# Loading the context already turned, and sharing the first norm between VectorE and ScalarE

## The chip, the cores and the metric

The kernel runs on one core of one Trainium2 chip. The metric is the device time of one execution in microseconds (us). Engines are TensorE (PE in the profile), VectorE (DVE), ScalarE (ACT), GpSimd (POOL) and SyncE (SP); SP and ScalarE both issue DMA transfers here.

## The reference

Four blocks are added to x one after the other. x and the context have shape (8, 256, 512) in float32. Only the start of the first block is touched:

```
def _layernorm(x, axis=-1, eps=1e-05):
    m = jnp.mean(x, axis=axis, keepdims=True)
    v = jnp.var(x, axis=axis, keepdims=True)
    return (x - m) / jnp.sqrt(v + eps)

# block 1: k = v = context, q = layernorm(x), head_dim 8, so 32 heads over the 256 positions
kv = jnp.einsum('bhil,bhjl->bijhl', k_, v_)
y = causal convolution of kv with ssm_kernel[h] along l (512 features), by FFT
out = einsum('bijhl,bhil->bjhl', y + kv * D, q_)
x = x + _L0_xattn_ref(ctx_2048, ctx_2048, _layernorm(x), ssm_kernel, D, 8)
# block 2: expert-choice routing FFN, block 3: retention, block 4: gated FFN with LoRA experts
```

The convolution runs along the 512 features, so x and the context are needed with the features on the partitions, that is, transposed from how they lie in memory.

## The kernel before

x has 2048 tokens, in 16 tiles of 128 tokens by 512 features (`TILES`), handled in 4 groups of 4 (`GROUP`). The stage before the convolution, here called stage A, makes two buffers with the features on the partitions: `ct` (the context) and `qt` (the norm of x). Both are seen as 32 blocks m (four blocks of 128 features times 8 batches) of 256 positions; `head_cols(t, h)` takes the 8 positions of head h from each block.

ScalarE first issues four loads of x, one per group, into `xres`. SP issues the constants, the taps and `d_heads`, then sixteen loads of one context tile each into four buffers `cin`, each when the transposes of the tile four before are done, and behind the first four the write of the taps into `toep`, from which the Toeplitz strips of the convolution are read (`strip_of`). The three first strips and the weights of block 2 (`ewf` and others) are issued behind the last context tile.

For each group TensorE turns four context tiles (banks 0 to 3) and four tiles of `xn` (banks 4 to 7), with `turn`: four transposes of 128x128. ScalarE copies every turned tile out of PSUM, first the four of `ct` and then the four of `qt`. VectorE works the norm of x by groups: `ln_stats` takes the statistics of four tiles (line 286), their aggregates (291) and adds eps (294), then waits until GpSimd has raised the variance to the power -1/2 (`ln_rstd`, line 305); `ln_apply` (299) writes four tiles of `xn`, each when the buffer is free.

At the end of the stage every engine waits for `END_A`: all copies into `ct` and `qt` done. Then ScalarE writes `kx` for heads 0 to 2 and `qx` for head 0 (`doubled`, line 620), GpSimd multiplies `kv` from `kx` (`kv_of`, lines 488 and 491), TensorE runs head after head with 20 products of strip and kv (line 939), ScalarE spreads the result (`spread`), VectorE and GpSimd multiply with `qx` (lines 1366, 1368, 502) and VectorE sums into `qt` (1372). Everything is ordered by semaphores; each engine works its own list in order.

Behind the convolution blocks 2 to 4 follow. The stage just behind it already works its norm by pairs of tiles (`pair`, `pair_root`, `apply`): statistics of two tiles on VectorE, power and product on GpSimd, application on ScalarE (line 669).

Of the kernel before, what the change touches and what calls it, by code (L numbers as in the profile page):

```python
# [13 lines left out]
F32 = mybir.dt.float32  # L14
F32R = mybir.dt.float32r
I32 = mybir.dt.int32
ALU = mybir.AluOpType
# [3 lines left out]
P = 128  # L21
# [4 lines left out]
GROUP = 4  # L26
# [27 lines left out]
def build(nc, x, ctx_in, taps, d_heads, consts, bits, rw, rb, ew, eb, wh, decay, wg, wo, gb,  # L54
          wr, ag, au, bd, spread, chunk_w, out):
    xr = x.rearrange("b (s p) d -> (b s) p d", p=P)
    cr = ctx_in.rearrange("b (s p) d -> (b s) p d", p=P)
    toep = nc.dram_tensor("toep", (HEADS, P + DIM), F32)
# [11 lines left out]
    with stack:  # L70
        start_of, primed = {}, []

        def sem(name, start=0):


            s = stack.enter_context(nc.semaphore(name))
            if start:
                start_of[s.name] = start
                primed.append((s, start))
            return s  # L80

        def sems(name, n, start=0):
            return [sem(f"{name}{i}", start) for i in range(n)]
# [8 lines left out]
        def place(spot, *buffers):  # L92

            made = []
            for name, shape, dt in buffers:
                t = nc.alloc_sbuf_tensor_at(name, shape, dt, offset=spot)
                n = 4
                for s in shape[1:]:
                    n *= s
                spot += -(-n // 32) * 32  # L100
                made.append(t)
            assert spot <= BASE + 212832
            return made
# [19 lines left out]
            ("kern", [HEADS, P + DIM], F32), ("dcol", [HEADS, 1], F32))  # L123
        cin, = place(W_AT + 1024, ("cin", [P, GROUP, DIM], F32))

# [87 lines left out]

        ln = {st: {k: sem(f"{st}_{k}", 1 if k == "xn" else 0) for k in ("stats", "var", "rstd", "xn")} for st in "AE"}
        x_in, c_in = sems("x_in", 4), sems("c_in", 4, 16)
        ctx_turned, ct_copied = sem("ctx_turned", GROUP), sem("ct_copied", GROUP)
        xa_turned, qt_copied = sem("xa_turned", GROUP), sem("qt_copied", GROUP)
# [50 lines left out]
        def raised(s):  # L268

            return start_of.get(s.name, 0)  # L270
# [48 lines left out]
        def after(eng, ends):  # L319

            for s, v in ends:
                eng.wait_ge(s, raised(s) + v)
# [11 lines left out]

        END_A = [(ct_copied, TILES), (qt_copied, TILES), (xa_turned, TILES)]
        END_CONV = [(conv_out, HEADS)]
# [35 lines left out]
        def _(sp):  # L372
# [3 lines left out]
            sp.dma_start(dcol[:, :], d_heads).then_inc(kern_in, 16)  # L376
            for g in range(GROUPS):
                for j in range(GROUP):
                    sp.wait_ge(c_in[j], raised(c_in[j]) + 16 * g)
                    sp.sem_inc(passed, 1)  # L380
                    sp.wait_ge(ctx_turned, raised(ctx_turned) + GROUP * g + j + 1 - GROUP)
                    sp.sem_inc(passed, 1)
                    sp.dma_start(cin[:, j, :], cr[GROUP * g + j]).then_inc(c_in[j], 16)
                if g == 0:
                    sp.wait_ge(kern_ready, 1)
                    sp.dma_start(bass.AP(toep, 0, [[P + DIM, HEADS], [1, P + DIM]]), kern[:, :]).then_inc(toep_written, 16)
            sp.wait_ge(toep_written, 16)
            for h in range(3):
                sp.dma_start(strip[:, h, :], strip_of(h)).then_inc(strip_in[h], 16)

            for dst, src in ((ewf[:, :, :], ew), (rwf[:, :, :], rw.rearrange("p (k e) -> p k e", k=KB)), (rbb[:, :], rb), (ebb[:, :], eb), (bitc[:, :], bits)):
                sp.dma_start(dst, src).then_inc(wB_in, 16)
# [81 lines left out]
        def _(pool):  # L474
# [3 lines left out]
            pool.wait_ge(s_set, 1)  # L478
            ln_rstd(pool, "A")
            after(pool, END_A)  # L480

# [120 lines left out]
        def _(act):  # L602
            for g in range(GROUPS):
                act.dma_start(xres[:, GROUP * g:GROUP * g + GROUP, :],
                              xr[GROUP * g:GROUP * g + GROUP].rearrange("t p d -> p t d")).then_inc(x_in[g], 16)
            for g in range(GROUPS):
                for j in range(GROUP):
                    act.wait_ge(ctx_turned, raised(ctx_turned) + GROUP * g + j + 1)
                    act.activation(turned(ct, GROUP * g + j), split(banks[:, j, :]),
                                   ACT.Copy).then_inc(ct_copied, 1)  # L610
                for j in range(GROUP):
                    act.wait_ge(xa_turned, raised(xa_turned) + GROUP * g + j + 1)
                    act.activation(turned(qt, GROUP * g + j), split(banks[:, 4 + j, :]),
                                   ACT.Copy).then_inc(qt_copied, 1)
            after(act, END_A)

# [5 lines left out]

            def doubled_k(h):
                if h >= 2:
                    act.wait_ge(kv_ready, h - 1)
                doubled(kx, ct, h).then_inc(kx_ready, 1)
# [289 lines left out]
        def _(pe):  # L916
            pe.wait_ge(s_const, 16)
            with pe.Fori(0, GROUPS, 1) as g:
                for j in range(GROUP):
                    pe.wait_ge(c_in[j], raised(c_in[j]) + 16 * (g + 1))  # L920
                    pe.wait_ge(ct_copied, raised(ct_copied) + GROUP * g + j + 1 - GROUP)
                    turn(pe, j, split(cin[:, j, :]), ctx_turned)
                for j in range(GROUP):
                    pe.wait_ge(ln["A"]["xn"], raised(ln["A"]["xn"]) + GROUP * g + j + 1)
                    pe.wait_ge(qt_copied, raised(qt_copied) + GROUP * g + j + 1 - GROUP)
                    turn(pe, 4 + j, split(xn[:, j, :]), xa_turned)
            after(pe, END_A)
# [413 lines left out]
        def _(dve):  # L1341
# [6 lines left out]
            dve.tensor_tensor(kern[:, P - 1:P], kern[:, P - 1:P], dcol[:, :], ALU.add).then_inc(kern_ready, 1)  # L1348
            for g in range(GROUPS):
                dve.wait_ge(x_in[g], 16)  # L1350
                ln_stats(dve, "A", g, lambda j: xres[:, GROUP * g + j, :], lambda j: None, EPS)
                for j in range(GROUP):
                    dve.wait_ge(xa_turned, raised(xa_turned) + GROUP * g + j + 1 - GROUP)
                    ln_apply(dve, "A", j, xres[:, GROUP * g + j, :])
            after(dve, END_A)
# [535 lines left out]
```

## Time and profile before

| | us |
|---|---|
| median of 3 timed runs | 1159.79 |
| the three runs | 1153.96, 1159.79, 1159.83 |
| the profiled execution | 1154.15 |
| its span in the profile | 1152.3 |
| busy: TensorE, VectorE, GpSimd, ScalarE | 1068.2, 624.1, 588.8, 440.6 |
| first product of the convolution starts | 39.99 |
| granted TensorE clock, mean over the profiled run | 0.972 |

The profile lists one execution. Times in its rows are us from the start of the span, unless a column says ns. A granted clock of 1.00 is TensorE's full 2.4 GHz, one of 0.50 is 1.2 GHz.

### The profile page before, as it was taken

How to read it: one execution, taken by the hardware profiler on the slowest of the kernel's cores; microseconds unless marked ns; L12 is line 12 of the kernel's file. 1: busy time of each engine (PE TensorE's matmuls, PEld its weight loads, DVE VectorE, ACT ScalarE, POOL GpSimd, SP SyncE). 2: the span in 40 equal slices, each digit the busy share in tenths (PEclk: the TensorE clock that was granted, in tenths of full speed). 3: DMA queues.
4: the chain of work that ended last, by engine and by line, in shares of the span. 5: the costliest groups of instructions: out<-in, count | busy, mean ns of one | idle time of the engine just before them, and what ended most of it. 6: DMA issues, size and time to landing. Idle time of an engine off the chain costs nothing.

```text
span 1152.3 us, 13470 instructions
## 1 busy us (share of the span) xinstructions
PE 1068.2 (93%) x4924; PEld 863.7 (75%) x4924; DVE 624.1 (54%) x1046; ACT 440.6 (38%) x803; POOL 588.8 (51%) x402
## 2 busy tenths in 40 slices
PE   5799998588889985999999999999999999999997
PEld 4577776465568864778668888888888888888886
DVE  6399999846875637756552352423424244242223
ACT  5354444441184535443532332333332232233222
POOL 1588996120032203230227676766776677667662
PEclk9899999888999988999999999999999999999999
DMA  8222121000010012000322212252323432232211
GB/s 306 92 55 64 56 56 28 1 1 1 1 37 1 1 74 97 1 1 1 165 89 87 96 69 87 78 185 105 116 74 107 155 132 80 95 113 87 71 67 37
DMA packets 24560, 85.47 MB, mean 74 GB/s; under 512 B 3169, under 2 KB 3825, under 8 KB 23729
## 3 DMA queue, kind: packets, MB, share of 16 engines
q1 hardware_dynamic: 22384, 80.45, 20.6%
q10 hardware_dynamic: 2112, 4.19, 1.0%
q8 instruction: 38, 0.62, 0.2%
q14 instruction: 26, 0.20, 0.1%
HBM read 74.85 MB, written 9.78 MB: 73 GB/s over the span
## 4 chain that ended last, share of the span: by engine, by line
PE 73%; DVE 19%; issue 4%; ACT 2%; POOL 1%; POOLq 0%; DVEq 0%; ACTq 0%
PE banks L315 23%; PE banks L316 22%; PE banks L317 22%; DVE qt L1372 6%; DVE pr L1366 6%; PE banks L310 3%; DVE pr L1368 1%; DVE stat L1390 1%; DVE junk L1466 1%; PE banks L939 1%; ACT xn L669 1%; PE banks L993 1%; PE banks L1187 0%; DVE xn L299 0%; DVE xtl L1402 0%
## 5 line engine op out<-in xcount | busy, mean ns | idle before, releaser
L1774 DVE TENSOR_TENSOR hf<-banks,silu 128x512 f32<-128x512 f32 x132 | 91.3, 692 | 323.5 <-PE banks L317 322.2
L582 POOL TENSOR_TENSOR gul<-wst,guh 128x1280 fp32r<-128x1280 f32 x44 | 129.9, 2952 | 141.7 <-DVE guh L1672 135.8
L592 POOL TENSOR_TENSOR hl<-hf,hh 128x512 fp32r<-128x512 f32 x129 | 178.2, 1412 | 8.6 <-ACT hh L897 8.6
L939 PE MATMUL banks<-kv,strip 128*128 128x288 f32 x640 | 158.4, 412 | 4.1 <-POOL kv L491 4.1
L897 ACT ACTIVATE hh<-hf 128x512 fp32r<-128x512 f32 x132 | 83.6, 633 | 190.0 <-DVE hf L1774 190.0
L939 PEld LDWEIGHTS banks<-kv,strip 128*128 128x128 f32 x640 | 123.4, 193 | 39.0 <-issue 4.4
L895 ACT ACTIVATE silu<-banks 128x512 f32<-128x512 f32 x132 | 78.9, 598 | 167.4 <-PE banks L317 167.2
L315 PE MATMUL banks<-xf,guh 128*128 128x512 f32 x352 | 137.2, 390 | 0.8 <-POOL gul L582 0.8
L316 PE MATMUL banks<-xf,guh 128*128 128x512 f32 x352 | 137.0, 389 | 0.0
L317 PE MATMUL banks<-xf,gul 128*128 128x512 f32 x352 | 136.9, 389 | 0.0
L525 POOL TENSOR_TENSOR rstd<-vare,mhalf 128x2 f32<-128x2 f32 x24 | 20.2, 842 | 150.7 <-DVE vare L1398 150.7
L587 POOL TENSOR_TENSOR dnl<-wst,dnh 128x640 fp32r<-128x640 f32 x44 | 68.9, 1566 | 42.6 <-DVE dnh L1769 42.6
L315 PEld LDWEIGHTS banks<-xf,guh 128*128 128x128 f32 x352 | 66.1, 188 | 15.8 <-POOL gul L582 1.3
L317 PEld LDWEIGHTS banks<-xf,gul 128*128 128x128 f32 x352 | 66.1, 188 | 13.7
L316 PEld LDWEIGHTS banks<-xf,guh 128*128 128x128 f32 x352 | 66.1, 188 | 13.5
L1366 DVE TENSOR_TENSOR pr<-banks,qx 128x1024 f32<-128x1024 f32 x32 | 65.2, 2038 | 16.5 <-ACT yx L643 15.8
L1372 DVE TENSOR_REDUCE qt<-pr 128x256 f32<-128x2048 f32 x32 | 73.2, 2286 | 1.1
L502 POOL TENSOR_TENSOR pr<-yx,qx 128x768 f32<-128x768 f32 x32 | 59.7, 1866 | 27.0 <-ACT yx L643 21.0
L310 PE MATMUL banks<-cst,xn 128*128 128x128 f32 x320 | 50.0, 304 | 24.9 <-DVE xn L299 12.3
L315 PE MATMUL banks<-rhl,guh 128*128 128x512 f32 x176 | 68.7, 390 | 0.4 <-ACT silu L895 0.3
L315 PE MATMUL banks<-dnh,hh 128*128 128x512 f32 x176 | 68.8, 391 | 0.0
L317 PE MATMUL banks<-rhl,gul 128*128 128x512 f32 x176 | 68.5, 389 | 0.0
(281 smaller groups left out, 2284.3 us busy)
## 6 DMA issues: line engine op xcount, KB each, us to landing
wst<-in_chunk_w SPq DMA_DIRECT2D x44, 960.0 KB, 4.7
strip<-toep SPq DMA_DIRECT2D x32, 256.0 KB, 3.2
xres<-in_x ACTq DMA_DIRECT2D x4, 1024.0 KB, 13.1
cin<-in_ctx SPq DMA_DIRECT2D x16, 256.0 KB, 5.7
xf_s<-xf SPq DMA_DIRECT2D x2, 2048.0 KB, 6.3
out<-xres SPq DMA_DIRECT2D x16, 256.0 KB, 2.1
xf<-xf_s SPq DMA_DIRECT2D x8, 512.0 KB, 5.9
mk<-hot_s SPq DMA_DIRECT2D x14, 256.0 KB
```

The source lines that it names most:

```text
L310: i = pe.transpose(banks[:, bank, k * P:(k + 1) * P], src[:, k, :], ident)
L315: pe.matmul(dst, wh_, mh_, start=first, stop=False, skip_group_check=check)
L316: pe.matmul(dst, wh_, ml_, start=False, stop=False, skip_group_check=check)
L317: return pe.matmul(dst, wl_, mh_, start=False, stop=last, skip_group_check=check)
L582: pool.tensor_tensor(gul[:, u, :], wst[:, u, 0:GU_W], f(guh[:, u, :]), ALU.subtract).then_inc(gul_ready, 1)
L592: pool.tensor_tensor(hl[:, u, s, :], hf[:, s, :], f(hh[:, u, s, :]), ALU.subtract)\
L895: act.activation(silu[:, s % 2, :], banks[:, 6, :], ACT.Silu).then_inc(silu_done, 1)
L897: act.activation(hh[:, u, s, :], hf[:, s, :], ACT.Copy).then_inc(hh_ready, 1)
L939: mm = pe.matmul(dst, strip[:, h % 3, far:far + P], view(kv, h % 3, m * BATCH * PAIRS, [[PAIRS, BATCH], [1, PAIRS]]), start=m == 0, stop=m ...
L1366: dve.tensor_tensor(view(pr, u, 0, [[HD * HD, MB], [1, 4], [HD, HD]]), rows, view(qx, u, 0, [[2 * HD, MB], [1, 4], [1, HD]]), ALU.mult)
L1372: dve.tensor_reduce(head_cols(qt, h), view(pr, u, 0, [[HD * HD, MB], [HD, HD], [1, HD]]), X_AXIS, ALU.add).then_inc(conv_out, 1)
L1774: dve.tensor_tensor(hf[:, s, :], banks[:, 7, :], silu[:, s % 2, :], ALU.mult).then_inc(mul_done, 1)
```

## The change

The host hands the context over with the features first, as two halves of positions 0 to 127 and 128 to 255 of each batch, and each half is one load straight into `ct`, in pieces of 128 floats. ScalarE issues both behind its four loads of x. The buffers `cin`, the transposes of context on TensorE and their copies on ScalarE are gone. SP goes on to `toep` and the strips at once, and waits for the second half before it loads the weights of block 2.

The norm of x goes by pairs n of tiles 2n and 2n+1. VectorE takes the statistics, GpSimd the power and the product with minus the mean. ScalarE applies the norm to every tile t but those with t % 4 == 2, which VectorE applies after the statistics of the next pair. Rows of statistics are reused from pair n by pair n+2. ScalarE copies the turned tiles of pair n-1 after applying pair n, and makes `kx` of heads 0 and 1 among the last pairs. GpSimd no longer waits for `END_A`, whose first condition is now the first half of the context.

```diff
-            for g in range(GROUPS):
-                for j in range(GROUP):
-                    sp.wait_ge(c_in[j], raised(c_in[j]) + 16 * g)
-                    sp.wait_ge(ctx_turned, raised(ctx_turned) + GROUP * g + j + 1 - GROUP)
-                    sp.dma_start(cin[:, j, :], cr[GROUP * g + j]).then_inc(c_in[j], 16)
...
+            sp.wait_ge(ct_in[1], 16)
             for dst, src in ((ewf[:, :, :], ew), ...):
                 sp.dma_start(dst, src).then_inc(wB_in, 16)
...
-            ln_rstd(pool, "A")
-            after(pool, END_A)
+            for n in range(TILES // 2):
+                s = slice(2 * (n % 2), 2 * (n % 2) + 2)
+                pool.wait_ge(lx_var, n + 1)
+                pool.tensor_tensor(rstd[:, s], vare[:, 0, s], mhalf[:, s], ALU.pow).then_inc(lx_pow, 1)
+                pool.wait_ge(lx_pow, n + 1)
+                pool.tensor_tensor(nmr[:, s], vare[:, 1, s], rstd[:, s], ALU.mult).then_inc(lx_rstd, 1)
...
+            for half in range(2):
+                act.dma_start(ct[:, :].rearrange("p (m c) -> p m c", m=MB)[:, :, half * P:(half + 1) * P], ctx_in[half])\
+                    .then_inc(ct_in[half], 16)
+
+            def apply_x(n):
+                act.wait_ge(lx_rstd, n + 1)
+                for t in (2 * n, 2 * n + 1):
+                    j = t % GROUP
+                    if j != 2:
+                        act.wait_ge(xa_turned, raised(xa_turned) + t + 1 - GROUP)
+                        act.activation(xn[:, j, :], xres[:, t, :], ACT.Identity,
+                                       bias=nmr[:, j:j + 1], scale=rstd[:, j:j + 1]).then_inc(xa_act, 1)
+
+            def keep_q(t):
+                act.wait_ge(xa_turned, raised(xa_turned) + t + 1)
+                act.activation(turned(qt, t), split(banks[:, 4 + t % GROUP, :]), ACT.Copy).then_inc(qt_copied, 1)
...
             def doubled_k(h):
+                if h == 0:
+                    act.wait_ge(ct_in[0], 16)
+                if h == HEADS // 2:
+                    act.wait_ge(ct_in[1], 16)
...
-            for h in range(3):
-                doubled_k(h)
+            apply_x(0)
+            for n in range(1, TILES // 2):
+                apply_x(n)
+                keep_q(2 * n - 2)
+                keep_q(2 * n - 1)
+                if n >= TILES // 2 - 2:
+                    doubled_k(n - TILES // 2 + 2)
+            keep_q(TILES - 2)
+            keep_q(TILES - 1)
+            after(act, END_A)
             doubled_q(0)
+            doubled_k(2)
...
+            for t in range(TILES):
+                if t % GROUP == 2:
+                    pe.wait_ge(xa_vec, t // GROUP + 1)
+                else:
+                    pe.wait_ge(xa_act, t + 1 - (t + 2) // GROUP)
+                pe.wait_ge(qt_copied, raised(qt_copied) + t + 1 - GROUP)
+                turn(pe, 4 + t % GROUP, split(xn[:, t % GROUP, :]), xa_turned)
...
+            for n in range(TILES // 2):
+                s = 2 * (n % 2)
+                if n % 2 == 0:
+                    dve.wait_ge(x_in[n // 2], 16)
+                if n >= 2:
+                    dve.wait_ge(xa_act, 2 * n - 2 - (n - 1) // 2)
+                for j in range(2):
+                    i = dve.bn_stats(stat6[:, s + j, :], xres[:, 2 * n + j, :])
+                i.then_inc(lx_stats, 1)
...
+                if n >= 1:
+                    apply_x(n - 1)
+            apply_x(TILES // 2 - 1)
             after(dve, END_A)
...
-        ("ctx", a["ctx_2048"].reshape(BATCH, SEQ, KB, P)[..., ::-1].reshape(BATCH, SEQ, DIM))
+        ("ctx", a["ctx_2048"].reshape(BATCH, SEQ, KB, P)[..., ::-1].transpose(3, 2, 0, 1).reshape(P, MB, 2, P).transpose(2, 0, 1, 3))
```

## Rows read from the trace of the kernel before

**Rows 1.** The page: the chain that ended last, by engine.

```profile
PE 73%; DVE 19%; issue 4%; ACT 2%; POOL 1%; POOLq 0%; DVEq 0%; ACTq 0%
```

**Rows 2.** The chain of waits in order of time, 30 to 50 us.

```profile
32.31 3.64 PE banks L310 x16
...
35.97 0.60 ACT qt L613
...
37.54 1.89 POOL kv L488
...
39.99 8.10 PE banks L939 x20
```

**Rows 3.** The timeline, 3 to 27 us: start, length, engine, line.

```profile
3.40 1.28 ACT L609 ACT_TABLE_LOAD   x1 [3.40 <-issue]
...
7.75 0.15 DVE L1348 TENSOR_TENSOR kern<-kern,dcol 32x1 f32<-32x1 f32 x1 [3.27 <-DMA dcol<-in_d_heads]
...
20.67 2.47 DVE L286 BATCH_NORM_STATS2 stat<-xres 128x6 f32<-128x512 f32 x4
...
21.55 2.06 ACT L613 ACTIVATE qt<-banks 128x512 f32<-128x512 f32 x4
...
25.01 1.92 DVE L299 TENSOR_SCALAR xn<-xres,mom,rstd 128x512 f32<-128x512 f32 x4 [1.13 <-POOL rstd L305]
...
27.05 2.47 DVE L286 BATCH_NORM_STATS2 stat<-xres 128x6 f32<-128x512 f32 x4
```

**Rows 4.** The chain of waits inside the convolution.

```profile
54.27 2.04 DVE pr L1366
...
59.12 2.04 DVE pr L1366
```

**Rows 5.** Groups of ScalarE instructions: busy us, mean ns, idle before.

```profile
L669 ACT ACTIVATE xn<-xres,nmr,rstd 128x512 f32<-128x512 f32 x48 | 36.4, 810 | 30.0 <-POOL nmr L527 29.9
...
L609 ACT ACTIVATE ct<-banks 128x512 f32<-128x512 f32 x16 | 9.1, 620 | 11.5 <-PE banks L310 11.5
```

**Rows 6.** The timeline of pairs in the stage behind the convolution.

```profile
209.10 1.19 POOL L525 TENSOR_TENSOR rstd<-vare,mhalf 128x2 f32<-128x2 f32 x1 [7.52 <-DVE vare L1398]
...
216.55 1.28 DVE L1390 BATCH_NORM_STATS2 stat<-xres 128x6 f32<-128x512 f32 x2
...
218.29 1.28 DVE L1378 TENSOR_TENSOR xres<-xres,banks 128x512 f32<-128x512 f32 x2
218.46 0.70 POOL L525 TENSOR_TENSOR rstd<-vare,mhalf 128x2 f32<-128x2 f32 x1 [3.16 <-DVE vare L1398]
...
219.47 1.52 ACT L669 ACTIVATE xn<-xres,nmr,rstd 128x512 f32<-128x512 f32 x2 [1.26 <-POOL nmr L527]
```

**Rows 7.** The tile xres, 0 to 40 us: its loads, and issue to landing.

```profile
L604 ACTq DMA_DIRECT2D xres<-in_x x4: 474/527/1016, 0.7 to 2.4; - x4
...
DMA to landing us min/median/max: 6.8/13.1/18.7
```

**Rows 8.** The DMA queues from 20 to 22 us: GB/s by slice, packets, share.

```profile
DMA packets 417, 0.76 MB, mean 381 GB/s; under 512 B 45, under 2 KB 45, under 8 KB 417
...
q1 hardware_dynamic: 392, 0.73, 98.8%
```

**Rows 9.** The DMA queues from 593.5 to 594.5 us, in 40 slices.

```profile
GB/s 0 0 0 0 0 0 0 0 0 0 0 123 123 102 184 205 225 205 246 266 123 225 226 82 123 62 82 21 0 0 0 0 0 0 0 0 82 82 102 143
...
q1 hardware_dynamic: 164, 0.08, 32.1%
...
L428 SPq DMA_DIRECT2D hot_s<-hot x4: 593/650/2027, 589.7 to 593.2; - x4
```

**Rows 10.** DMA issues from 0 to 60 us: KB each, us to landing.

```profile
toep<-kern SPq DMA_DIRECT2D x1, 80.0 KB, 5.6
```

**Rows 11.** Windows before and in head 0; PEclk is third from the end.

```profile
33.00:34.00 1.00, 1.00 (x6) 1.00 (x5) 0.62 (x2) 0.59 (x1) 0.00 (x0) 0.50 0.94 351
...
40.00:46.00 6.00, 6.00 (x13) 4.28 (x14) 0.00 (x0) 1.21 (x4) 4.36 (x4) 0.50 0.00 0
```

More of the change, by code:

```diff
@@ L56, in build @@
     xr = x.rearrange("b (s p) d -> (b s) p d", p=P)
-    cr = ctx_in.rearrange("b (s p) d -> (b s) p d", p=P)
     toep = nc.dram_tensor("toep", (HEADS, P + DIM), F32)
@@ L123, in build @@
             ("kern", [HEADS, P + DIM], F32), ("dcol", [HEADS, 1], F32))
-        cin, = place(W_AT + 1024, ("cin", [P, GROUP, DIM], F32))
         xth, = place(XH_AT, ("xth", [P, KB * TOKENS], F32R))
@@ L212, in build @@
         passed = sem("passed")
-        ln = {st: {k: sem(f"{st}_{k}", 1 if k == "xn" else 0) for k in ("stats", "var", "rstd", "xn")} for st in "AE"}
-        x_in, c_in = sems("x_in", 4), sems("c_in", 4, 16)
-        ctx_turned, ct_copied = sem("ctx_turned", GROUP), sem("ct_copied", GROUP)
+        ln = {st: {k: sem(f"{st}_{k}", 1 if k == "xn" else 0) for k in ("stats", "var", "rstd", "xn")} for st in "E"}
+        x_in, ct_in = sems("x_in", 4), sems("ct_in", 2)
+        lx_stats, lx_var, lx_pow, lx_rstd, xa_vec, xa_act = (
+            sem(n) for n in ("lx_stats", "lx_var", "lx_pow", "lx_rstd", "xa_vec", "xa_act"))
         xa_turned, qt_copied = sem("xa_turned", GROUP), sem("qt_copied", GROUP)
@@ L333, in heads @@
             weigh(RHEADS - 1)
-        END_A = [(ct_copied, TILES), (qt_copied, TILES), (xa_turned, TILES)]
+        END_A = [(ct_in[0], 16), (qt_copied, TILES), (xa_turned, TILES)]
         END_CONV = [(conv_out, HEADS)]
@@ L376, in _ @@
             sp.dma_start(dcol[:, :], d_heads).then_inc(kern_in, 16)
-            for g in range(GROUPS):
-                for j in range(GROUP):
-                    sp.wait_ge(c_in[j], raised(c_in[j]) + 16 * g)
-                    sp.sem_inc(passed, 1)
-                    sp.wait_ge(ctx_turned, raised(ctx_turned) + GROUP * g + j + 1 - GROUP)
-                    sp.sem_inc(passed, 1)
-                    sp.dma_start(cin[:, j, :], cr[GROUP * g + j]).then_inc(c_in[j], 16)
-                if g == 0:
-                    sp.wait_ge(kern_ready, 1)
-                    sp.dma_start(bass.AP(toep, 0, [[P + DIM, HEADS], [1, P + DIM]]), kern[:, :]).then_inc(toep_written, 16)
+            sp.wait_ge(kern_ready, 1)
+            sp.dma_start(bass.AP(toep, 0, [[P + DIM, HEADS], [1, P + DIM]]), kern[:, :]).then_inc(toep_written, 16)
             sp.wait_ge(toep_written, 16)
@@ L605, in _ @@
                               xr[GROUP * g:GROUP * g + GROUP].rearrange("t p d -> p t d")).then_inc(x_in[g], 16)
[L606 to L615, printed above, removed]
+            for half in range(2):
[12 more added lines that the diff above has]
+                act.activation(turned(qt, t), split(banks[:, 4 + t % GROUP, :]), ACT.Copy).then_inc(qt_copied, 1)
             def doubled(dst, src, h):
@@ L917, in _ @@
             pe.wait_ge(s_const, 16)
[L918 to L926, printed above, removed]
+            for t in range(TILES):
[5 more added lines that the diff above has]
+                turn(pe, 4 + t % GROUP, split(xn[:, t % GROUP, :]), xa_turned)
             after(pe, END_A)
@@ L1348, in _, with apply_x @@
             dve.tensor_tensor(kern[:, P - 1:P], kern[:, P - 1:P], dcol[:, :], ALU.add).then_inc(kern_ready, 1)
[L1349 to L1354, printed above, removed]
+            def apply_x(n):
+                t = 2 * n
+                if t % GROUP == 2:
+                    dve.wait_ge(lx_rstd, n + 1)
+                    dve.wait_ge(xa_turned, raised(xa_turned) + t + 1 - GROUP)
+                    dve.tensor_scalar(xn[:, 2, :], xres[:, t, :], mom[:, 2, 0:1], rstd[:, 2:3],
+                                      ALU.subtract, ALU.mult).then_inc(xa_vec, 1)
+            for n in range(TILES // 2):
[7 more added lines that the diff above has]
+                i.then_inc(lx_stats, 1)
+                dve.wait_ge(lx_stats, 2 * n + 1)
+                for j in range(2):
+                    i = dve.bn_aggr(mom[:, s + j, :], stat6[:, s + j, :])
+                i.then_inc(lx_stats, 1)
+                dve.wait_ge(lx_stats, 2 * n + 2)
+                dve.tensor_scalar(vare[:, 1, s:s + 2], mom[:, s:s + 2, 0], -1.0, None, ALU.mult)
+                dve.tensor_scalar(vare[:, 0, s:s + 2], mom[:, s:s + 2, 1], EPS, None, ALU.add).then_inc(lx_var, 1)
+                if n >= 1:
+                    apply_x(n - 1)
+            apply_x(TILES // 2 - 1)
             after(dve, END_A)
@@ L1866 @@
     values = [
-        ("x", a["x"]), ("ctx", a["ctx_2048"].reshape(BATCH, SEQ, KB, P)[..., ::-1].reshape(BATCH, SEQ, DIM)), ("taps", taps),
+        ("x", a["x"]), ("ctx", a["ctx_2048"].reshape(BATCH, SEQ, KB, P)[..., ::-1].transpose(3, 2, 0, 1).reshape(P, MB, 2, P).transpose(2, 0, 1, 3)), ("taps", taps),
         ("d_heads", a["L0_xattn_D"].reshape(HEADS, 1)), ("consts", consts), ("bits", bits),
```

## The prediction

> **What bounds the kernel now.** I read the page first. Its chain that ended last is 73% TensorE and 19% VectorE, nearly all of it in work that the diff does not touch, so this change can only move the point at which that work starts [rows 1]. I then read the chain of waits in order of time over the first 50 us, to find what the convolution, the first stage behind the edit, starts on. It runs backwards from the first convolution product: 39.99 waits for GpSimd's kv product (from 37.54), that for ScalarE's doubled kx, that for the last copy into qt at 35.97, and that for sixteen transposes of xn, which took 3.64 [rows 2]. Ahead of them stands a VectorE loop of 6.39 us per four tiles, which the timeline shows (two starts of the statistics, 20.67 and 27.05): four statistics 2.47, their aggregates and one add, 1.13 waiting for GpSimd's power, four applications 1.92 [rows 3]. From the convolution on the period is VectorE's: 4.85 us a head (54.27 to 59.12), with pr and qt back to back [rows 4]. A head start is therefore carried through all 32 heads and on to the end, unless a clock or a transfer takes it back. So the question is how far before 39.99 the first head can start.
>
> **The change part by part.** Sixty-four transposes of context and sixteen ScalarE copies of them (mean 620 ns, 9.1 us busy) vanish [rows 5]. They were not on the path by themselves, since VectorE's loop was. That loop now splits: VectorE keeps the statistics and four of sixteen applications, ScalarE takes twelve.
>
> *VectorE and GpSimd per pair.* The same pair code already runs behind the convolution, so its price is read there. Statistics start at 216.55 and the instruction behind the pair at 218.29: 1.75 us a pair. GpSimd's power starts at 218.46 and ScalarE at 219.47, so an application can start 1.2 us after VectorE is done [rows 6]. Four VectorE applications of 0.54 each make VectorE's total 8 x 1.75 + 4 x 0.54 = 16.2 us, against 4 x 6.39 = 25.6.
>
> *ScalarE.* Two applications take 1.52 together [rows 6], one alone 0.81 [rows 5], two copies 1.1 (0.49 between starts, as four took 2.06 [rows 3], then a full 0.60 [rows 2]). Two pairs cost ScalarE 1.52 + 1.1 + 0.81 + 1.1 = 4.5 us, VectorE 2 x 1.75 + 0.54 = 4.0. ScalarE is the new bound of the stage, by a small margin.
>
> *The start.* VectorE still waits for the taps and d_heads, until 7.75 [rows 3]; the first group of x had landed by 0.7 + 6.8 = 7.5 [rows 7]. Statistics at 7.9, the pair done at 9.65, and then 1.2 plus the 0.5 by which a first power is slower (1.19 against 0.70 [rows 6]): ScalarE at 11.3. Pair 2 reuses the slot of pair 0 and waits for its applications (12.8); VectorE 1.75, GpSimd 1.2, ScalarE at 15.7, one us of it lost to that wait.
>
> *The sum.* From 15.7 two rounds of 4.5 lead to 24.7, the applications of pair 6. Then 1.5 + 1.1 for them and the copies, at 27.3 the doubled kx of head 0 (0.7) to 28.0, one application 0.8, two copies 1.1, kx of head 1 0.7, two last copies 1.1: 31.7. GpSimd makes kv of head 0 from 28.1 to 30.5, under these. So the first head starts at 31.8 in place of 39.99: 8.2 us earlier. Some 4.9 of it is the stage (last copy 36.57 to 31.7), the rest is the 3.4 of kx, kv and their handovers that no longer follow the last copy. The new doubling of kx 2 behind qx 0 costs nothing: GpSimd and TensorE are in heads 0 and 1 (8.1 us) meanwhile.
>
> *x arrives in time.* The queues moved 381 GB/s when full [rows 8]. x with the small constants is 4.5 MB: from about 2.2 (my estimate, 1.5 behind the first issue) it is through at 14.0. Its groups land near 7.5, 10, 12.8 and 15.5 (adding 1.5 for landing), wanted at 7.9, 12.8, 17.3 and 21.9. SP's ring carries the toep write (5.6 from issue to landing [rows 10], so 13.5) and three strips, now issued there instead of behind all of context: 0.8 MB more, to 16.1. They are wanted at 31.8.
>
> *Context in pieces of 512 bytes.* Each half is 4096 such pieces, 256 per DMA engine, and is wanted at 27.3. The store of hot writes such pieces (128 floats each): 164 packets, 32.1% of 16 engines over 1 us, that is 31 ns each, where a 2 KB packet took 0.988 x 2 x 16 / 392 = 81 ns [rows 8, 9]. At 31 ns a half takes 8.0 us: done at 24.1, landed by 25.6, 1.7 before need. The bound below is the full rate, 5.5 us. Above, that store's burst (128 packets in 14 slices of 25 ns [rows 9]) would make it 11.2 us, landing at 28.8, 1.5 late; and if a short piece costs as much as a long one, 20.7 us, landing at 38.3, 11.0 late. I take 31, the nearest row, and keep the others for the range. The second half is wanted by head 16, some 75 us later, and by SP for the ew loads, which ScalarE reads after head 5; both have room.
>
> By the Trainium skill's page DMA: Bandwidth & Descriptors, section Why small descriptors are slow, each packet costs about 3 cycles besides its 32-byte beats. That is 19 cycles against 67, so my estimate from that page and the 81 ns row is 23 ns and 5.9 us per half. The row shows more than the rule; by either the half is there before it is wanted, and the sum would be the same.
>
> *Issuing on ScalarE.* Both context transfers are issued by the engine that must apply the norm. Its four x issues took 0.47 to 1.02 each [rows 7], for 512 packets of 2 KB, and the table load behind them began at 3.40 [rows 3]; a store of hot took 0.59 or more for 128 packets [rows 9]. The time goes little by packets, so I take 1 us each: ScalarE is free at 3.4 + 2 + 1.3 (table load) = 6.7, and 11.3 is the need. If it goes by packets ((3.40 - 0.7) / 4 = 0.67 per 512), it is 10.7 for both, free at 15.4, 4.1 late.
>
> *The clock.* Head 0 took 8.10, at a granted clock of 0.50 from 40 to 46, where a steady head takes 4.85 [rows 2, 4, 11]. In the run-up the grant had fallen to 0.50 during the last sixteen transposes and TensorE then sat idle for 4 us [rows 11]. After the change TensorE has half as many transposes and waits shorter before head 0. I price head 0 at 8.1 as now; at full clock 3.2 more would be won, at half clock all through about 1.5 lost. Nothing else hangs on the edit: cin's space is not used otherwise here.
>
> The profiled execution took 1154.15 us (span 1152.3). Less 8.2 this is 1146.0. The three timed runs were 1153.96, 1159.79 and 1159.83, so the profile sits with the faster one, and the median is 5.6 above it. A median of several new runs may fall at either level, 1146.0 or 1151.6; I forecast 1150.5, nearer the upper, where two of three lay.
>
> **The rivals.** (a) *ScalarE is held by its own DMA issues; slower.* The queue to the DMA engines may hold no more than has been seen in it, about the 2048 packets of x. Then the last issue ends only when half of the second context half is left: 16.1 + 8.0 + 4.0 = 28.1, plus the table load 29.4. From there the stage needs 31.8 - 11.3 - 1.0 = 19.5: the first head starts at 48.9, 8.9 late, 1163.0 on the profiled scale. Break-even is ScalarE free at 20.5. For it: the fourth x issue took twice the first. Against: that one ended at 3.36, long before x had drained, so no limit was met yet.
>
> The Trainium skill's page Perfetto Trace Analysis, section DMA Instruction — HWDGE (DVE, Sync), speaks for this rival. It says that the reported time of such an instruction covers the exclusive use of the descriptor generator, and that more descriptors can be made than the buffer holds. This trace has no DMA with so many packets, so it bears out neither side; by the page's rule with a buffer that x just fills, the time is that of (a), without it the sum above.
>
> (b) *The issues go by packets:* ScalarE 4.1 late, gain 4.1, 1150.1 profiled, inside half a per cent. (c) *The short pieces are late:* 1.5 to 11.0 late at kx of head 0, which also stands before the last application in ScalarE's order, so all of it is passed on; gain 6.7 down to a loss of 2.8. (d) *The head start is lost later,* because TensorE meets the search and norm stages behind the convolution at another moment of its clock, whose mean grant over the whole run is 0.972, below full: a shift either way of 2 or 3 us.
>
> **How the numbers follow.** About half a per cent, 5.8 us, is what a measurement of this kernel can tell from no change. Forecast 0.57; (a) 0.12; (b) 0.12; (c) 0.12; (d) by itself 0.07. The forecast and part of (c) and (d) are faster: 0.62. (b), most of (c) and half of (d) are within: 0.26. (a) is slower: 0.12. The range goes from the faster level with a warmer first head (1146.0 less 2) to the upper level with a gain of nearly nothing: 1144 to 1158.5. It leaves out (a) and the best case of the clock.
>
> **What would show it.** Right: kv starts under the last copies into qt; the first head at about 32; ScalarE without idle time over 0.5 us from 16 on; the ct issues done before 8 us; the first half landed by 26; period and length of everything after it unchanged. Wrong: ScalarE's first application well after 11.3, with an issue before it (a or b); ScalarE waiting for ct at kx of head 0 (c); VectorE waiting for GpSimd in its statistics; a first head longer than 8.1 us, or the start at 32 but an end that moved by less than 6 (d).

## The result

The changed kernel takes 1157.51 us (median of 20 runs), the kernel before 1152.97 (20 runs): a ratio of 1.0035, 95% interval 1.0021 to 1.0048. It is a little slower, by an amount inside the half per cent that the prediction called indistinguishable. The interval does not hold 1, so with 20 runs of each kernel the loss stands clear of the noise, which is narrower than that half per cent. The range held the time, but the sign was wrong: the forecast was 1150.5 us, a gain of 8.2 us on the profiled scale, with 0.62 for faster.

The timeline of the changed kernel's first 42 us answers to [rows 2, 3]:

```profile
3.28 16.14 ACTq L603 DMA_DIRECT2D ct<-in_ctx  x2
...
9.63 0.70 POOL L474 TENSOR_TENSOR rstd<-vare,mhalf 128x2 f32<-128x2 f32 x1 [6.22 <-DVE vare L1386]
...
19.51 1.28 ACT L612 ACT_TABLE_LOAD   x1 [19.51 <-issue]
20.81 2.22 ACT L612 ACTIVATE xn<-xres,nmr,rstd 128x512 f32<-128x512 f32 x3
...
22.43 1.29 DVE L1378 BATCH_NORM_STATS2 stat<-xres 128x6 f32<-128x512 f32 x2 [11.21 <-ACT xn L612]
...
41.58 10.67 PE L952 MATMUL banks<-kv,strip 128*128 128x288 f32 x43 [1.56 <-ACT qt L617]
```

The first row sets the stage. ScalarE's two context issues take from 3.28 to 19.42. GpSimd has its first power at 9.63 and could have let ScalarE start at 10.6; ScalarE loads its table at 19.51 and applies the norm for the first time at 20.81. VectorE sat idle for 11.21 us in its third pair, waiting for the slot that ScalarE had not read. The convolution starts at 41.58, 1.6 later than the 39.99 of [rows 2]. The tile ct shows the two issues apart (shortest, median, longest in ns) and how long the halves took to land:

```profile
L603 ACTq DMA_DIRECT2D ct<-in_ctx x2: 2971/8054/13136, 3.3 to 6.3; - x2
...
DMA to landing us min/median/max: 20.5/23.0/25.6
```

2.97 and 13.14 us, where [rows 7] had 0.47 to 1.02 for an issue of x. The first half landed at 3.28 + 20.5 = 23.8, before the 27.3 at which the prediction wanted it. The DMA queue of ScalarE from 16 to 22 us:

```profile
q10 hardware_dynamic: 179, 1.47, 81.0%
```

A packet here holds sixteen short pieces: 0.810 x 6 x 16 / 179 = 434 ns for 8.2 KB, so 27 ns a piece. That lies between the 31 of the row of hot and the 23 that the prediction estimated with the Trainium skill's page DMA: Bandwidth & Descriptors, section Why small descriptors are slow; the measurement decides, and either was good enough.

A 1.6 us later convolution does not make 4.5 us. The execution above is the fastest of the twenty (1154.78). A second profile of the same kernel, e10 of the experiments, took 1159.47 (span 1157.7), the slowest of its five; the medians lie between the two. The first head of the second profile ran at a low clock, like that of the kernel before, and in both profiles two places far behind the edit have more low clock than the kernel before. Windows of the second profile, the last three columns granted clock, DMA share and GB/s:

```profile
41.00:48.00 7.00, 6.11 (x13) 4.43 (x14) 0.00 (x0) 2.13 (x6) 4.51 (x4) 0.51 0.02 5
464.00:472.00 8.00, 6.79 (x18) 5.38 (x19) 6.69 (x14) 4.42 (x13) 2.09 (x2) 0.57 0.00 0
570.00:574.00 4.00, 4.00 (x13) 1.92 (x14) 2.03 (x3) 1.45 (x3) 1.00 (x1) 0.57 0.02 4
```

of the first profile, where head 0 ran at full clock,

```profile
41.00:47.00 6.00, 5.42 (x23) 4.30 (x24) 0.00 (x0) 2.11 (x6) 4.19 (x4) 1.00 0.02 5
460.00:466.00 6.00, 5.45 (x13) 4.29 (x14) 5.71 (x13) 3.09 (x9) 0.45 (x2) 0.50 0.00 0
566.00:569.00 3.00, 3.00 (x9) 1.03 (x8) 2.05 (x3) 0.75 (x2) 0.68 (x1) 0.52 0.02 5
```

and of the kernel before, where the same work lies:

```profile
39.00:47.00 8.00, 7.01 (x17) 5.12 (x18) 0.00 (x0) 1.33 (x4) 5.36 (x6) 0.57 0.00 0
462.00:466.00 4.00, 2.97 (x7) 2.40 (x8) 4.00 (x6) 0.62 (x2) 0.90 (x1) 0.57 0.02 4
466.00:472.00 6.00, 6.00 (x28) 4.92 (x28) 4.69 (x14) 5.08 (x15) 1.01 (x1) 1.00 0.00 0
570.00:574.00 4.00, 4.00 (x26) 3.40 (x25) 1.29 (x2) 1.57 (x3) 2.23 (x1) 1.00 0.00 0
```

The buffers vh, uh and xf are written by ScalarE in later stages and serve as marks here; their times are the starts of their last writes.

| us, from the timelines | before | changed, second profile | difference | changed, first profile | difference |
|---|---|---|---|---|---|
| convolution starts | 39.99 | 41.90 | 1.9 | 41.58 | 1.6 |
| head 0 done | 48.1 | 50.0 | 1.9 | 46.7 | -1.4 |
| last vh (line 732 before) | 416.1 | 417.9 | 1.8 | 413.5 | -2.6 |
| last uh (line 821 before) | 534.9 | 538.6 | 3.7 | 533.9 | -1.0 |
| last xf (line 832 before) | 572.5 | 577.8 | 5.3 | 573.1 | 0.6 |
| end of the span | 1152.3 | 1157.7 | 5.4 | 1153.0 | 0.7 |

In the second profile 1.9 us come from the start and 3.5 from two stretches in which TensorE was granted 1.2 GHz for longer than in the kernel before: near 465 to 471 and 570 to 573. The first profile loses nearly the same there, 3.2 us from the last vh to the last xf, at about 460 to 466 and 566 to 569. It ends only 0.7 late because its head 0 was 3.0 us shorter than that of the kernel before, and 1.2 more were gained on the way to the last vh; where, was not followed up.

### The profile page after: what moved, and what is told of

Read it like the earlier page. It is cut to its first block, busy times and chain, and to the rows that moved or that the text cites. A ratio compares the mean times of both kernels' runs of the same rounds, so it can differ in the third digit from the quotient of the medians.

```text
span 1153.0 us, 13248 instructions
## 1 busy us (share of the span) xinstructions
PE 1061.9 (92%) x4860; PEld 857.2 (74%) x4860; DVE 620.1 (54%) x1046; ACT 439.9 (38%) x799; POOL 592.6 (51%) x414
## 3 DMA queue, kind: packets, MB, share of 16 engines
q1 hardware_dynamic: 20080, 76.25, 19.5%
## 4 chain that ended last, share of the span: by engine, by line
PE 73%; DVE 19%; ACT 2%; issue 1%; POOL 1%; DVEq 0%; POOLq 0%; ACTq 0%
PE banks L314 23%; PE banks L316 22%; PE banks L315 22%; DVE qt L1407 6%; DVE pr L1401 6%; PE banks L309 3%; DVE pr L1403 1%; DVE junk L1501 1%; DVE stat L1425 1%; ACT xn L684 1%; PE banks L1200 1%; PE banks L1006 1%; PE banks L952 0%; DVE xn L298 0%; PE banks L1053 0%
## 5 line engine op out<-in xcount | busy, mean ns | idle before, releaser
L952 PE MATMUL banks<-kv,strip 128*128 128x288 f32 x640 | 155.4, 406 | 1.6 <-ACT qt L617 1.6
L309 PE MATMUL banks<-cst,xn 128*128 128x128 f32 x320 | 53.3, 317 | 47.5 <-ACT xn L612 22.5
L309 PEld LDWEIGHTS banks<-cst,xn 128*128 128x128 f32 x320 | 42.9, 163 | 59.5 <-issue 39.3
L314 PEld LDWEIGHTS banks<-xf,guh 128*128 128x128 f32 x352 | 66.1, 188 | 15.6 <-POOL gul L578 1.3
```

The costliest lines, as they stand in the source:

```text
L309: i = pe.transpose(banks[:, bank, k * P:(k + 1) * P], src[:, k, :], ident)
L314: pe.matmul(dst, wh_, mh_, start=first, stop=False, skip_group_check=check)
L952: mm = pe.matmul(dst, strip[:, h % 3, far:far + P], view(kv, h % 3, m * BATCH * PAIRS, [[PAIRS, BATCH], [1, PAIRS]]), start=m == 0, stop=m ...
```

## The experiments

All comparisons are with the kernel before on the same chip. "Start" is the first product of the convolution in the profile.

### Who issues the context

e1 moves both issues to SP, behind the first strips; e2 only the second.

```diff
-            for half in range(2):
-                act.dma_start(ct[...half...], ctx_in[half]).then_inc(ct_in[half], 16)
...
             for h in range(3):
                 sp.dma_start(strip[:, h, :], strip_of(h)).then_inc(strip_in[h], 16)
+            sp.dma_start(ct[...0...], ctx_in[0]).then_inc(ct_in[0], 16)
+            sp.dma_start(ct[...1...], ctx_in[1]).then_inc(ct_in[1], 16)
```

> The changed kernel with one edit: both halves of context are issued by SP behind the first three strips, not by ScalarE. Theory A (ScalarE was held by its second context issue, 6.3 to 19.4 us, and the rest of the first stage is as the sum of the prediction has it): ScalarE's first application at about 11.3 instead of 20.8, first product of the convolution at 31 to 33.5 instead of 41.6 (33.5 if the first half, landed by 24 to 27, comes late for kx), SP itself held in its second issue until about 20. Time 8 to 9 us under the changed kernel, ratio to the kernel before 0.994 to 0.997. Rival B (it is not the hold; the loads share the queues with x and the stage is late for another reason): first application still after 18, convolution after 40, ratio 1.003. Rival C (the head start is made, but the clock of TensorE in the later stages takes it back, since the changed kernel was 2.5 us ahead at 450 us and 0.6 behind at 600): convolution at 32, but the time within 3 us of the kernel before.

> The changed kernel with one edit: ScalarE issues the first half of context, SP the second behind the strips. Theory A1 (a limit on what waits: the first issue was let through with about 2.9 MB of x in 2 KB pieces and 4096 pieces of context waiting, some 5,500 pieces, and the second ended when the waiting pieces had fallen to about the same number): the issue on ScalarE takes 3.0 us, ScalarE is free at 7.6 with the table load, first application at 11.3, convolution at 31 to 33; SP's issue is held or not, which costs nothing. Rival A2 (any issue of 4096 pieces holds its engine until x has drained, and the first was let go only because the generator was empty): first application after 14. Theory A1 gives a ratio to the kernel before of 0.994 to 0.997, Rival C (clock later takes it back) 0.998 to 1.002.

e1 takes 1144.19 us, ratio 0.9929 (0.9917 to 0.9942); e2 1144.60, 0.9927 (0.9914 to 0.9940). They gain 8 to 9 us on the kernel before and 13 on the changed one. That is more than either expectation had (a ratio of 0.994 to 0.997, for e1 8 to 9 us under the changed kernel): the start moved by 10.2 us, and e1's profile also has the two later stretches as short as the kernel before. Rivals B and C have fallen. The timeline of e1, with SP's and ScalarE's rows:

```profile
3.32 1.28 ACT L613 ACT_TABLE_LOAD   x1 [3.32 <-issue]
...
10.59 1.52 ACT L613 ACTIVATE xn<-xres,nmr,rstd 128x512 f32<-128x512 f32 x2 [5.99 <-POOL nmr L480]
...
13.73 0.68 SPq L381 DMA_DIRECT2D ct<-in_ctx  x1
...
14.44 7.07 SPq L383 DMA_DIRECT2D ct<-in_ctx  x1
...
15.37 1.52 ACT L613 ACTIVATE xn<-xres,nmr,rstd 128x512 f32<-128x512 f32 x2 [1.29 <-POOL nmr L480]
...
27.30 0.71 ACT L623 ACTIVATE kx<-ct 128x256 f32<-128x256 f32 x2
...
31.37 20.84 PE L953 MATMUL banks<-kv,strip 128*128 128x288 f32 x78 [1.94 <-ACT qt L618]
```

First application at 10.59, kx of head 0 at 27.30 and the start at 31.37 stand against 11.3, 27.3 and 31.8 in the sum of the prediction. So with the issue moved the sum comes within 0.7 us at each step, in part because errors cancel (below). Now SP is held (7.07 us in its second issue), and nobody waits for it. In e2 the start is 31.53. ScalarE's one issue took 3.03, as theory A1 had it, and SP's, with a queue of its own, 0.68; A2, which had the first application after 14, has fallen:

```profile
3.42 3.03 ACTq L604 DMA_DIRECT2D ct<-in_ctx  x1
...
10.75 1.52 ACT L613 ACTIVATE xn<-xres,nmr,rstd 128x512 f32<-128x512 f32 x2 [2.93 <-POOL nmr L478]
...
13.79 0.68 SPq L381 DMA_DIRECT2D ct<-in_ctx  x1
```

### Longer pieces, issued by ScalarE

e3 hands context over with all 32 blocks of a partition together, so that each of ScalarE's two loads has 16 KB per partition in one piece, and kx of head 0 waits for both.

```diff
-                act.dma_start(ct[...half...], ctx_in[half])
+                cols = slice(part * KB * TOKENS // 2, (part + 1) * KB * TOKENS // 2)
+                act.dma_start(ct[:, cols], ctx_in[:, cols]).then_inc(ct_in[part], 16)
```

> The changed kernel with context handed over so that each partition's 32 KB of ct lie together: ScalarE issues two loads with pieces of 8 KB or more, and kx of head 0 waits for both. Theory A1 (the hold goes by pieces): both issues together under 2 us, ScalarE free at about 6.5 with the table load; DMA at 380 to 390 GB/s instead of 290 to 306 in the context loads; both landed at 27 to 29, so kx of head 0 about 1 late, convolution at 32 to 34. Rival (the hold goes by bytes waiting, about 4.9 MB at the end of the second issue): the second issue is held until about 10 us, ScalarE free at 11 to 12, convolution at 33 to 35. Ratio to the kernel before 0.993 to 0.998 by either.

1146.99 us, ratio 0.9951 (0.9939 to 0.9964). The issues of ct:

```profile
L604 ACTq DMA_DIRECT2D ct<-in_ctx x2: 734/1868/3002, 3.4 to 6.4; - x2
...
DMA to landing us min/median/max: 17.7/19.0/20.3
```

The second issue fell from 13.1 to 0.73 us at the same bytes: the hold does not go by bytes. The first stayed at 3.00, so that both took 3.77 together where I had expected under 2. The start is 31.56, as in e1, yet the time is 2.8 us longer than e1's; the shifted kernels below bear on that difference.

### Each half of the change alone

e5 takes the kernel before and only loads the context by feature (ScalarE one half, SP the other); e6 takes the changed kernel with context loaded by tiles, turned and copied as before, between the pairs of the shared norm.

```diff
 e5, on the kernel before
-                    turn(pe, j, split(cin[:, j, :]), ctx_turned)
-                    act.activation(turned(ct, GROUP * g + j), split(banks[:, j, :]), ACT.Copy)
+            act.dma_start(ct[...0...], ctx_in[0]).then_inc(ct_in[0], 16)
+            sp.dma_start(ct[...1...], ctx_in[1]).then_inc(ct_in[1], 16)
...
 e6, on the changed kernel
                 apply_x(n)
+                if n < TILES // 2 - 1:
+                    keep_c(2 * n + 2)
+                    keep_c(2 * n + 3)
                 keep_q(2 * n - 2)
```

> The kernel before with the context half of the change alone: context loaded by feature (first half issued by ScalarE, second by SP behind the strips, so that ScalarE is not held), and x normed by groups of four as before, with kx of heads 0 to 2 behind the last copy as before. If VectorE's loop of 6.4 us per group sets the first stage, taking away sixteen transposes and sixteen copies of context gives nothing: convolution at 39 to 40.5, time within 3 us of the kernel before. Rival (the copies of context on ScalarE were on the path): convolution 4 us or more earlier.

> The changed kernel with the norm half of the change alone: context loaded by tiles by SP, turned by TensorE and copied by ScalarE as in the kernel before, interleaved with the shared norm by pairs; kx of head 0 between the last pairs. ScalarE then has 12 applications, 32 copies and kx, about 12 x 0.76 + 32 x 0.53 + 1.4 = 27.5 us from 11 on, so the convolution starts at 38 to 40 and the norm alone gives at most 1 to 2 us. Rival (ScalarE fits the copies into its waits): convolution at 35 or earlier, 4 us gained without the new loads.

e5: 1153.59 us, ratio 1.0008 (0.9994 to 1.0022), start 39.91. e6: 1155.19 us, 1.0025 (1.0012 to 1.0037), start 41.18. Their first products:

```profile
39.91 12.48 PE L927 MATMUL banks<-kv,strip 128*128 128x288 f32 x42 [4.06 <-POOL kv L483]
```

```profile
41.18 11.14 PE L976 MATMUL banks<-kv,strip 128*128 128x288 f32 x38 [3.40 <-POOL kv L496]
```

Neither half gives anything, and the norm half alone loses 2.5 us. Taking the copies of context from ScalarE frees an engine that was not the bound; giving it the applications without taking the copies makes it the bound: in e6 ScalarE had no idle time from 19.5 to 39.6. e6 started 1.2 us later than the latest that I had expected, since four copies of context stand ahead of its first application, which came at 14.88. Together, and with the issues moved, they give 8 to 9 us.

### Does only the start count?

e4 is e2 with six copies before ScalarE's first application, which nothing needs; e7, e8 and e9 put one or two of them into the changed kernel; e10 is the changed kernel again.

```diff
+            act.wait_ge(lx_rstd, 1)
+            for idle, width in ((pr[:, 0, :], 2048), ...):
+                act.activation(idle[:, 0:width], xres[...], ACT.Copy)
             apply_x(0)
```

> The kernel with one context issue on ScalarE and one on SP, and before ScalarE's first application six copies into buffers that are unused then, about 8.2 us of work that nothing needs, so that the whole first stage comes that much later and the convolution starts near 40 as in the kernel before. If only the start of the convolution counts, its time is 8.2 us over the kernel without the copies and within 1.5 us of the kernel before. Rival C (what happens behind depends on where TensorE's clock changes fall, not on the start alone): its time differs from both by another amount, up to 5 us either way.

> The changed kernel (both context issues on ScalarE) with one copy of 512 elements that nothing needs before ScalarE's first application: everything behind comes about 0.6 us later. In the runs so far the time less the end of head 0 was 1110.8 for the changed kernel and 1105.0 to 1107.6 for the kernel before and the four experiments. Theory P (how long TensorE's half-clock stretches last behind the convolution depends on where they fall against the work, so the extra 5 us of the changed kernel belong to its start time and not to its code): a shift of 0.6 us need not add 0.6; the time may fall by several us, to 1152 to 1156, or stay. Rival S (the changed kernel is slower behind the convolution for a fixed reason, as its loads): the time rises by 0.6, to 1158.

> The same with one copy of 2048 elements, about 1.8 us later. Theory P: anywhere from 1153 to 1160, and not in line with the other shifts. Rival S: 1.8 over the changed kernel, 1159.3.

> The same with copies of 2048 and 1152 elements, about 3 us later. [...] Rival S: 3.0 over the changed kernel, 1160.5. [...]

> The changed kernel itself on the chip of the shifted ones, for their baseline and for a second profile. Expected 1156 to 1159; in the profile the half-clock stretches behind 400 us should again be longer than in the kernel before (about 459 to 467 and one near 565) if they are a property of the start time, and elsewhere if they are chance.

| kernel | start | head 0 done | time | ratio to before (95%) |
|---|---|---|---|---|
| e4 | 39.35 | 46.2 | 1151.75 | 0.9989 (0.9976 to 1.0002) |
| e10 | 41.90 | 50.0 | 1157.42 | 1.0043 (1.0029 to 1.0056) |
| e7 | 42.19 | 47.3 | 1154.75 | 1.0017 (1.0006 to 1.0028) |
| e8 | 43.62 | 50.4 | 1155.39 | 1.0021 (1.0009 to 1.0032) |
| e9 | 44.57 | 51.4 | 1159.08 | 1.0051 (1.0034 to 1.0067) |

e4 confirms the main line: 7.8 us of later start than e2 cost 7.2, and a kernel with e2's code and nearly the old start has the old time. e7 adds work that nothing needs and is 2.7 us faster than e10, with intervals that just miss each other (1.0028 and 1.0029) and runs that do not overlap (1152.3 to 1156.4 against 1156.8 to 1159.5). e8 starts 1.7 later and is 2.0 faster, with intervals that overlap. The fixed-reason theory (rival S) has fallen: it wanted 0.6 and 1.8 more. e10 came out as expected, in its time and in its two long stretches. In e7's profile head 0 ran at full clock, which is worth 2.7 us against e10 at its end, and the windows that cost e10 its 3.5 us are short or gone:

```profile
42.00:48.00 6.00, 5.81 (x24) 4.63 (x25) 0.00 (x0) 2.11 (x6) 3.80 (x4) 1.00 0.02 5
460.00:464.00 4.00, 2.85 (x7) 2.30 (x8) 4.00 (x6) 0.49 (x2) 1.02 (x1) 0.57 0.00 0
464.00:468.00 4.00, 4.00 (x19) 3.29 (x18) 2.69 (x9) 4.00 (x13) 1.01 (x1) 1.00 0.00 0
566.00:570.00 4.00, 4.00 (x21) 3.06 (x20) 1.37 (x3) 0.87 (x2) 2.55 (x1) 1.00 0.00 0
```

e9's profile (1156.91) lacks the long stretches too, though its median is 1159.1; one profile is one draw.

The two stretches come in two lengths. From the last vh to the last xf the kernel before, e1, e2, e4, e5, e7, e8 and e9 took 156.3 to 156.6 us, and both profiles of the changed kernel, e3, e6, e11, e12 and e13 took 159.5 to 159.9, with none between. That is most of e3's 2.8 us over e1. The arrival time alone does not choose: with the last vh at 413.9 (e11) and 414.8 (e6) they were long, at 414.0 (e5) and 414.1 (e7) short.

One code can also take different times with its clock. Among 56 runs of the kernel before beside the experiments, the four with a mean granted clock of 0.975 took 1149.6 to 1150.1 us and the three with 0.966 or 0.967 took 1157.2 to 1158.4. All 25 runs of the changed kernel had 0.966 to 0.970.

### What lets a held issue go

e11 and e12 leave ScalarE a quarter and a half of the second half, with SP issuing the rest. e13 lets ScalarE issue two quarters of the first half.

```diff
+            act.dma_start(ct[...][:, 0:8, P:2 * P], ctx_in[1][:, 0:8, :]).then_inc(ct_in[1], 16)
...
+            sp.dma_start(ct[...][:, 8:32, P:2 * P], ctx_in[1][:, 8:32, :]).then_inc(ct_in[1], 16)
```

> The changed kernel, but of the second context half ScalarE issues only the first quarter (8 of 32 blocks, 1024 pieces of 512 bytes) and SP the rest behind the strips. Theory N (an issue ends when no more than about 5,640 pieces wait in its own queue: at 6.25 the changed kernel had 3.15 MB of x in 2 KB pieces and 4096 pieces of context waiting, 5,630; at 19.42 it had 2.90 MB of context, 5,660): the quarter is let through when x is down to about 520 pieces, 3.1 MB of it moved, so at about 11.6 us; ScalarE's first application at 12.9, convolution at 33 to 34. Rival G (a second issue is held until the first one's data has begun, or for a time that does not depend on its size): the quarter's issue ends at 14 or later, near 19 like the half's. Rival H (it costs generating time only, 0.7 ns a piece): it ends at 7 to 7.5, convolution at 31.5.

> The same with the first half of the second context half on ScalarE (16 of 32 blocks, 2048 pieces) and SP the rest. Theory N: 6144 pieces of context wait, so all of x and about 500 of them must have left: the issue ends at about 15.2, first application at 16.5, convolution at 36 to 37. Rival G: near 19. Rival H: at 8.

One run each: 1155.22 and 1156.86 us, where one run of the kernel before beside them took 1156.78; their times are not compared. ScalarE's second issue of e11, and then of e12:

```profile
6.58 13.20 ACTq L606 DMA_DIRECT2D ct<-in_ctx  x1
...
21.16 2.23 ACT L615 ACTIVATE xn<-xres,nmr,rstd 128x512 f32<-128x512 f32 x3
```

```profile
6.52 13.21 ACTq L606 DMA_DIRECT2D ct<-in_ctx  x1
```

13.20 and 13.21 us for 1024 and 2048 pieces, as for the 4096 of the changed kernel. Theory N, by which the new pieces count, is refuted (it had the issues end at 11.6 and 15.2, and starts of 33 to 37 where 41.93 and 41.88 came), and so are rival H and theory A1, which counted them too. Rival G, a hold that does not depend on the size, had it right here. What the releases have in common is what is left ahead in the same queue. The part of the queue moved by the first release, and left at the second, in the changed kernel:

```profile
q10 hardware_dynamic: 510, 1.04, 49.1%
```

```profile
q10 hardware_dynamic: 386, 2.90, 47.5%
```

2048 - 510 = 1,538 packets of x at the first; 2.90 MB less the 2.10 of the new load, so 0.80 MB or 1,560 pieces, at the second. The first issues of e2 and e4 ended with 1,499 and 1,516 packets of x left, and those of e3, e5, e11 and e12 with 1,496 to 1,528. The same sum for second issues gives 0.74 MB (1,440 pieces) in e11, 0.72 (1,400) in e12 and 0.64 (1,250) for SP's held issue in e1. e3's second issue fits if its long rows count as few pieces: 657 packets had moved at 7.14, which leaves 1,391 of x. That made theory Q, tested by e13:

> The changed kernel, but ScalarE issues two quarters of the first context half (1024 pieces each) and SP the rest behind the strips. The size of the held issue did not matter in the last two runs (13.2 us each), so theory N (counting the new pieces) has fallen. Theory Q, formed on the runs so far: an issue is let go when the pieces ahead of it in its own queue are down to about 1,500. At the release of the first context issue 1,500 to 1,540 packets of x were left in four kernels; at the release of the second 0.64 to 0.80 MB of the first half, 1,250 to 1,560 pieces. By Q the first quarter's issue ends at 6.2 to 6.6, and the second, with 1024 pieces and what is left of x ahead, when 3.2 MB of x have moved, at 11 to 12.5; first application at 12.5 to 14. Rival R (a second transfer of short pieces waits until about two thirds of the first have moved, whatever is ahead): x must be through first, so its issue ends at 15 to 16.5. Rival G (a fixed 13.2 us): at 19.8.

1150.58 us in one run. ScalarE's rows, and its queue until the second issue ended:

```profile
6.70 5.70 ACTq L608 DMA_DIRECT2D ct<-in_ctx  x1
12.49 1.28 ACT L617 ACT_TABLE_LOAD   x1 [12.49 <-issue]
13.79 2.22 ACT L617 ACTIVATE xn<-xres,nmr,rstd 128x512 f32<-128x512 f32 x3
```

```profile
q10 hardware_dynamic: 1580, 3.15, 75.2%
```

The second issue ended at 12.40 and the first application came at 13.79, both inside what Q said (11 to 12.5, 12.5 to 14) and outside R and G. The first ended at 6.67, just past Q's 6.2 to 6.6, with 1,498 packets of x left. Ahead of the second were 2048 - 1580 = 468 packets of x and 1024 pieces: 1,490. The start was 34.56. SP's two issues there bear Q out once more. The one of 2048 pieces took 0.67 us, and the one of 4096 behind it 5.52, let go at 20.56 with 0.80 MB (1,560 pieces) of the first left.

## Why the prediction was wrong

*The step that failed* is the one headed "Issuing on ScalarE": "The time goes little by packets, so I take 1 us each: ScalarE is free at ... 6.7". Measured, ScalarE was free at 19.42, and 20.8 with the table load. In its place the runs show that an issue does not end, and its engine does nothing else, until the queue ahead of it is down to some 1,250 to 1,560 pieces; x (2048 packets) and the first half (4096 pieces) are well over that. e1 and e2 move the issue and nothing else, and the start comes 10 us earlier and the time is 13 us shorter; that is shown, not argued. The 13 hold some 3 us of the low-clock stretches, which the moved issue does not explain by itself.

*The range* held by luck. Its upper end stood for the upper of two levels with a gain of nearly nothing, not for a held ScalarE, which it left out.

*Rival (a)* was the right mechanism at 0.12. Its size was off: it let the queue hold 2048 pieces including the new ones and had ScalarE free at 29.4. Its own break-even, ScalarE free at 20.5, was nearly met: it was free at 20.8, and the kernel came out just slower. The sentence used against it, that the fourth x issue "ended at 3.36, long before x had drained, so no limit was met yet", drew too much from the row. That issue, with 1,536 packets issued ahead of it, took 0.61 to 1.02 us in the traces, where the first took 0.47 to 0.49, and it ended when the first 5 to 29 packets of x had moved, with 1,507 to 1,531 left. That fits the limit of the later runs, but no run isolates it. The Trainium skill's page Perfetto Trace Analysis, section DMA Instruction — HWDGE (DVE, Sync), says that the reported time covers the making of all descriptors, which can be more than the buffer holds. The 13.14 us issue agrees; the size of the limit is this case's.

*Rival (b)*, issues that cost by packets, has fallen: 4096 pieces took SP 0.68 us in e1 and e2.

*The sum* came within 0.7 us at each step in e1, partly by luck. I took the first power at 1.19; it was 0.70, and the first application came 0.7 early. The round of two pairs took 4.78 us and not 4.5, since ScalarE waited 0.6 in each for GpSimd's product, and pair 2 came 4.8 behind pair 0 and not 4.4: 0.9 late in all. From pair 6 to the start it took 6.45 and not 7.1. From the release on, the changed kernel needed 41.6 - 20.8 = 20.8 against 19.5, where I had taken off the wait of pair 2: VectorE had gone idle after two pairs, and pair 2 waited for the slot here too.

*Context in short pieces* (c): priced at 31 ns, measured 27; landed at 23.8, in time in every run. The burst of [rows 9] fills 17 slices and not 14, so that bound was 53 ns a piece and 13.6 us; nothing came of it. *x in time*: its last group landed at 15.6, against 15.5.

*The clock* (d): priced at 2 or 3 us either way behind the convolution. It was 3.5 in the second profile, on top of 1.9 at the start, and 3.2 in the first, where a head 0 at full clock (5.1 us, 3.0 won, where the prediction had 3.2 for that case) and 1.2 more hid it. The shifted kernels show that the changed code with a little work added can lack the long stretches, so the code alone does not make them. What chooses between the two lengths is not settled here.

*The scale*: I set the forecast between two levels of three runs. Over 20 runs the median of the kernel before is 1152.97, and five of the 20 lie at 1158.0 to 1159.8: the upper level exists but is the rarer one, so the profile was typical and the three-run median was not.

## What to carry to other kernels

Before a load is given to an engine that computes, count the pieces that its queue will already hold, not the bytes, and read the longest issue of the trace against the shortest: here the one issue that took twice its neighbours' time stood at the limit. Put bulk loads of short runs on an engine whose next work is late, here SP. An edit that frees one engine and one that loads it can each be worth nothing and be worth 8 us together, so measure them together. The version to keep is e1: 1144.19 us, ratio 0.9929 (0.9917 to 0.9942) to the kernel before; e2 is not told apart from it.

## What the hardware showed

- An issue from ScalarE or SP was let go with 1,250 to 1,560 pieces left ahead in its own queue, in fourteen issues of nine kernels, whatever its own size (1024, 2048 or 4096 pieces: 13.20, 13.21 and 13.14 us). The queues of ScalarE and SP count apart: 0.68 us for 4096 pieces on SP while ScalarE's queue still held the 4096 of the first half (e2).
- Loads whose rows lie 512 bytes long in SBUF ran at 287 to 306 GB/s (changed kernel, 16 to 22 us), 27 ns a piece, against 387 to 393 for 2 KB rows (8 to 14 us).
- Two low-clock stretches of TensorE more than 400 us behind the edit came in two lengths, 3.2 us apart, in fifteen profiles. A kernel with 0.6 us of useless work more had the short ones and was 2.7 us faster (e7 against e10).
